# The opening of a three-layer decoder kernel: the attention pipeline filled by the rounds of its own loop, or by a program written out for each engine

## What is computed

```
x = LN(x + attn(x))        # LN, QKV, rotary; A = sum over tokens of l2(K)*V; Y = A*l2(Q); Y @ W_out + x
x = LN(x + xattn(ctx, x))  # 16 heads of 64: queries from x, keys and values from LN(ctx) and LN(x), softmax, @ Wo
x = LN(x + ffn(x))         # 8 experts of width 512, each token goes to its top 2
```

## Time and profile before

| | |
|---|---|
| time, three executions | 1606.64 us median (1605.07 to 1608.68) |
| profiled execution | 1606.26 us, span 1604.4 us |
| PE busy | 1432.5 us, 89% |
| DVE, ACT, POOL busy | 1105.5, 1031.7, 904.7 us |
| first matmul, first scores of tile 0 | 5.72 us, 76.38 us after the start of the span |

### The profile page before, as it was taken

How to read it: one execution, slowest core, us unless ns; L and a number is a source line. 1 busy time by engine, 2 the same in 40 slices (tenths; PEclk the granted TensorE clock), 3 DMA queues, 4 the chain that set the end, 5 groups by cost and what they waited for, 6 DMA issues and landing times.

```text
span 1604.4 us, 36488 instructions
## 1 busy us (share of the span) xinstructions
PE 1432.5 (89%) x10509; PEld 1239.7 (77%) x10509; DVE 1105.5 (69%) x4107; ACT 1031.7 (64%) x3827; POOL 904.7 (56%) x1233
## 2 busy tenths in 40 slices
PE   5699999999999999999999999999997499999940
PEld 4578888888888888888888888888886498889940
DVE  3366777767777677776777767777666588777865
ACT  2377776777767777677776777767764255555535
POOL 3355556665566665666556665566544255455565
PEclk9799999999999999999999999999999699999975
DMA  2000000000000000000000000000000676677746
GB/s 78 11 11 8 15 16 15 18 16 15 16 15 18 17 14 16 15 18 17 14 16 15 17 17 14 16 16 17 10 10 14 181 242 218 213 221 225 222 153 196
DMA packets 64624, 96.18 MB, mean 60 GB/s; under 512 B 10892, under 2 KB 48786, under 8 KB 64306
## 3 DMA queue, kind: packets, MB, share of 16 engines
q1 hardware_dynamic: 44738, 71.90, 15.0%
q0 software_dynamic: 8896, 16.94, 3.1%
q10 hardware_dynamic: 10800, 5.06, 1.2%
HBM read 71.55 MB, written 23.35 MB: 59 GB/s over the span
## 4 chain that ended last, share of the span: by engine, by line
PE 69%; DVE 10%; ACT 9%; DMA 4%; issue 4%; POOL 2%; SPq 2%; ACTq 0%; POOLq 0%; DVEq 0%
PE ps_s L1208 15%; PE ps_o L1221 11%; PE ps_t L1241 10%; ACT probs L607 6%; PE ps_pT L1231 5%; PE ps_t L1371 3%; PE ps_u L1256 3%; PE ps_a L1307 3%; PE ps_u L1258 3%; PE ps_u L1257 3%; DVE neg_max L759 3%; DVE pT L771 3%; PE ps_u L1371 2%; DVE k_pick L814 2%; DMA f_x<-x_rows 2%
## 5 line engine op out<-in xcount | busy, mean ns | idle before, releaser
L607 ACT ACTIVATE probs<-ps_s,neg_max 128x128 f32<-128x128 f32 x1024 | 361.8, 366 | 290.2 <-DVE neg_max L759 290.2
L496 POOL TENSOR_TENSOR probs_n<-probs,inv_sum 128x512 f32<-128x512 f32 x256 | 265.9, 1039 | 251.6 <-DVE inv_sum L765 249.6
L1208 PE MATMUL ps_s<-kvT,u_sb 128*128 128x128 f32 x2048 | 281.1, 280 | 0.0
L1208 PEld LDWEIGHTS ps_s<-kvT,u_sb 128*128 128x128 f32 x2048 | 255.2, 192 | 33.2 <-issue 31.8
L1241 PE MATMUL ps_t<-pT,kv_rows 128*128 128x512 f32 x512 | 262.2, 594 | 0.8 <-DVE pT L771 0.8
L1221 PE MATMUL ps_o<-value_w,tT 128*128 128x128 f32 x2048 | 260.5, 275 | 2.4 <-ACT tT L618 2.2
L759 DVE TENSOR_REDUCE neg_max<-ps_s 128x4 f32<-128x512 f32 x256 | 176.2, 688 | 103.9 <-PE ps_s L1208 103.4
L1221 PEld LDWEIGHTS ps_o<-value_w,tT 128*128 128x128 f32 x2048 | 244.0, 192 | 4.3 <-ACT tT L618 4.3
L553 POOL DMA_INDIRECT y_rows<-wvT,f_id x144 | 144.8, 1006 | 152.4 <-DVE wvT L1118 94.9
L607 ACT ACTIVATION_READ_ACCUMULATOR probs<-ps_s,neg_max 128x1 f32 x1024 | 208.2, 203 | 0.0
L508 POOL DMA_INDIRECT x_rows<-routed,pos_i x128 | 136.7, 1068 | 121.2 <-DVE pos_i L950 101.0
(11 more groups left out here) (237 smaller groups left out, 3165.6 us busy)
## 6 DMA issues: line engine op xcount, KB each, us to landing
u_sb<-in_expert_w SPq DMA_DIRECT2D x45, 578.0 KB
tT<-in_expert_w SPq DMA_DIRECT2D x27, 578.0 KB
f_x<-x_rows SPq DMA_DIRECT2D x72, 130.0 KB
tT<-y_rows SPq DMA_DIRECT2D x16, 512.0 KB, 4.7
x_raw<-in_x SPq DMA_DIRECT2D x64, 64.0 KB, 1.8
c_raw<-in_ctx_in SPq DMA_DIRECT2D x64, 64.0 KB, 2.0
out<-u_sb ACTq DMA_DIRECT2D x16, 256.0 KB, 2.4
y_rows<-wvT,f_id POOLq DMA_INDIRECT x144
```

Source lines behind the costliest of these rows:

```text
L496: nc.gpsimd.tensor_tensor(probs_n[:, sl], probs[:, sl], inv_sum[:, sl, :].rearrange("p (u o) -> p u o", o=1).to_broadcast([P, UP, P]), ALU ...
L607: last = nc.scalar.activation(probs[:, sl, j], ps_s[sl][:, j * P:(j + 1) * P], ACT.Exp, bias=neg_max[:, sl, j:j + 1], accum_out=sums[:, sl ...
L1208: last = nc.tensor.matmul(ps_s[sl][:, j * P:(j + 1) * P], u_sb[:, c // 2, BT * p + b, h:h + 2].rearrange("p h s -> p (h s)"), kvT[:, c, 2 ...
```

## The change

The periods start at t = 0. What the periods -5 to -1 did is written out, per engine, as one list of calls. In the lists, tiles 0 and 1 are treated side by side, then 2 and 3, then 4. To allow it, odd tiles below 5 (`FILL`) use `ps_o` in place of `ps_a`, tiles 2 and 3 use `ps_pT` for `KVT`, and the first eight latents parts alternate between `ps_u` and `ps_t`. The preparation jobs use five banks in place of seven and are strewn between the steps of the tiles. The score weights are split straight from the bank: ACT writes score_hi, DVE score_lo with one operation per job, in place of `split_scores`. The buffers for x and context are four each, their first loads stand in front of the large weights, and each constant has a semaphore that is awaited where it is first used. In the periods that remain three waits are new: `keep_qkv` for `sq_done`, `ctx_hat` for `kvT_ps`, and on PE `turn_latents` for `kvT_done` and `turn_rows_back` for `kv_done`; the wait for `score_split` is gone.

```diff
+        X_RING = 4
+        x_raw = sb("x_raw", [P, X_RING, D])
+        c_raw = sb("c_raw", [P, X_RING, D])
...
+        def chain_bank(j):
+
+            return ps_o if j < FILL and j % 2 else ps_a
...
+        def KVT(j):
+            return (ps_pT if 2 <= j < 4 else ps_u)[:, 0:BT * P]
+
+        def U_BANK(n):
+            return ps_t if n < 8 and n % 2 else ps_u
...
-        FIRST, LAST = -5, NT + 4
...
-            for t in range(FIRST, LAST + 1):
+            for t in range(LAST + 1):
...
+        ACT_JOBS = [0, 2, 4, 6, 7, 8, 9, 10, 11, 13]
+        DVE_JOBS = [1, 3, 5, 7, 8, 9, 10, 12, 14]
...
-            def load(j, q):
-                sp.wait_ge(z1_done, count(j - 1))
-                sp.wait_ge(c_hat_done, count(j - 1))
+            def load(j):
+                q = j % X_RING
+                sp.wait_ge(z1_done, count(j - (X_RING - 1)))
+                sp.wait_ge(c_hat_done, count(j - (X_RING - 1)))
                 sp.dma_start(x_raw[:, q:q + 1, :], x_t[one(j), :, :].rearrange("t p d -> p t d")).then_inc(x_in[q], 16)
...
             sp.dma_start(ident[:], eye).then_inc(s_ident, 16)
+            load(0)
             sp.dma_start(wq_raw[:], w_q).then_inc(s_wq, 16)
+            load(1)
             sp.dma_start(wkv_raw[:], w_kv).then_inc(s_wkv, 16)
-            load(0, 0)
             sp.dma_start(wo_raw[:], w_o.rearrange("(c p) n -> p c n", p=P)).then_inc(s_wo, 16)
-            sp.dma_start(tri[:], before).then_inc(s_const, 16)
-            sp.dma_start(eids[:], expert_ids).then_inc(s_const, 16)
-            sp.dma_start(rbase[:], region_base).then_inc(s_const, 16)
-            sp.dma_start(tids[:], tile_ids).then_inc(s_const, 16)
+            load(2)
+            load(3)
+            sp.dma_start(tri[:], before).then_inc(s_place, 16)
+            sp.dma_start(eids[:], expert_ids).then_inc(s_place, 16)
+            sp.dma_start(rbase[:], region_base).then_inc(s_place, 16)
+            sp.dma_start(tids[:], tile_ids).then_inc(s_place, 16)
...
+            load(4)
+            load(5)
...
+                if on(t, 6):
+                    load(t + 6)
...
+            def ctx_hat(j):
+                q = j % 2
+                pool.wait_ge(in_rstd, j + 1)
+                pool.wait_ge(kvT_ps, count(j - 1))
+                nc.gpsimd.tensor_scalar(c_hat[:, q], c_raw[:, j % X_RING], mv_in[:, q, 1, 0:1], rs_in[:, q, 1:2],
+                                        ALU.subtract, ALU.mult).then_inc(c_hat_done, 1)
...
             pool.wait_ge(half_set, 7)
-            pool.wait_ge(s_const, 16 * N_CONST)
-            pool.wait_ge(s_gains, 16 * N_GAINS)
+            in_rstds(0)
+            in_rstds(1)
+            ctx_hat(0)
+            ctx_hat(1)
+            qk_rstds(0)
+            qk_rstds(1)
+            in_rstds(2)
+            z1_rstds(0)
+            latent_hat(0)
+            z1_rstds(1)
+            latent_hat(1)
+            in_rstds(3)
+            qk_rstds(2)
+            ctx_hat(2)
+            ctx_hat(3)
+            z1_rstds(2)
+            qk_rstds(3)
+            latent_hat(2)
+            in_rstds(4)
+            z1_rstds(3)
+            latent_hat(3)
+            ctx_hat(4)
+            qk_rstds(4)
...
+                elif kind == "m":
+                    nc.scalar.activation(heads_of(g, score_hi[:]), bank[:].rearrange("p (c d) -> p c d", c=4), ACT.Copy,
+                                         scale=QS_SCALE).then_inc(prep_act, 1)
...
-            act.wait_ge(s_const, 16 * N_CONST)
-            act.wait_ge(s_gains, 16 * N_GAINS)
-            act.wait_ge(g_lat_set, 1)
```

ACT's list, which follows the definitions of its helpers:

```diff
+            keep_prepared(0)
+            act.wait_ge(s_norm, 32)
+            x_turned(0)
+            keep_prepared(2)
+            x_turned(1)
+            keep_qkv(0)
+            keep_prepared(4)
+            keep_qkv(1)
+            keep_prepared(6)
+            keep_prepared(7)
+            keep_prepared(8)
+            x_turned(2)
+            keep_prepared(9)
+            keep_qkv(2)
+            x_turned(3)
+            keep_prepared(10)
+            act.wait_ge(s_lat, 64)
+            act.wait_ge(g_lat_set, 1)
+            keep_kvT(0)
+            keep_prepared(11)
+            keep_qkv(3)
+            keep_kvT(1)
+            keep_prepared(13)
+            keep_u(0)
+            keep_rows(0)
+            keep_u(1)
+            keep_rows(1)
+            keep_u(2)
+            x_turned(4)
+            keep_u(3)
+            keep_u(4)
+            keep_qkv(4)
+            keep_u(5)
+            keep_kvT(2)
+            keep_u(6)
+            keep_u(7)
+            keep_kvT(3)
             periods(act, period)
```

DVE's split of the score weights, and its list:

```diff
+                if kind == "m":
+                    dve.wait_ge(prep_act, ACT_JOBS.index(at) + 1)
+                    nc.vector.scalar_tensor_tensor(heads_of(g, score_lo[:]), bank[:].rearrange("p (c d) -> p c d", c=4), QS_SCALE,
+                                                   heads_of(g, score_hi[:]).bitcast(F32), ALU.mult, ALU.subtract).then_inc(prep_dve, 1)
+                    return
...
+            stats(0)
+            stats(1)
+            in_hats(0)
+            keep_prepared(1)
+            in_hats(1)
+            dve.wait_ge(s_lat, 64)
+            nc.vector.tensor_scalar(g_lat[:], g_lat[:], (1 + EPS_LN) ** -0.5, None, ALU.mult).then_inc(g_lat_set, 1)
+            keep_prepared(3)
+            dve.wait_ge(s_rot, 48)
+            rotate(0)
+            keep_prepared(5)
+            pick(0)
+            rotate(1)
+            scale_queries(0)
+            stats(2)
+            pick(1)
+            residual(0)
+            keep_prepared(7)
+            scale_queries(1)
+            in_hats(2)
+            x1_norm(0)
+            residual(1)
+            keep_prepared(8)
+            stats(3)
+            x1_norm(1)
+            in_hats(3)
+            rotate(2)
+            keep_prepared(9)
+            pick(2)
+            keep_prepared(10)
+            split_latents(0)
+            rotate(3)
+            scale_queries(2)
+            keep_prepared(12)
+            split_latents(1)
+            keep_prepared(14)
+            residual(2)
+            pick(3)
+            stats(4)
+            x1_norm(2)
+            scale_queries(3)
+            in_hats(4)
+            residual(3)
+            dve.wait_ge(s_gate, 32)
+            dve.wait_ge(s_place, 64)
+            nc.vector.tensor_copy(tri_bf[:], tri[:]).then_inc(pad_ready, 1)
+            rotate(4)
+            x1_norm(3)
+            pick(4)
+            split_latents(2)
+            scale_queries(4)
             periods(dve, period)
```

PE's waits, two helpers and its list:

```diff
                 if at == TURNED:
-
-                    pe.wait_ge(prep_act, (TURNED + 1) // 2)
-                    pe.wait_ge(prep_dve, TURNED // 2)
+                    for kept in range(1, 5):
+                        pe.wait_ge(*prep_kept(kept))
+                if at == TURNED + 4:
...
-            for at in range(TURNED):
-                prepare(at)
-            pe.wait_ge(pad_ready, 5)
-            pe.wait_ge(s_const, 16 * N_CONST)
-            pe.wait_ge(s_gains, 16 * N_GAINS)
...
+            def latents_part(n):
+
+                pair = n // 8 % 2
+                if n % 4 == 0:
+                    tiles = min(n // 4 + 2, NT) if n >= 8 else 2
+                    pe.wait_ge(lT_done, tiles)
+                    pe.wait_ge(kvT_done, 3 * tiles)
+                pe.wait_ge(u_done, n if n >= 8 else count(n - 1))
...
+            def turn_latents(j):
+                pe.wait_ge(l_hat_done, j + 1)
+                pe.wait_ge(c_hat_done, j + 1)
+                pe.wait_ge(kvT_done, 3 * j)
+                nc.tensor.transpose(KVT(j)[:, 0:P], l_hat[:, j % 2], ident[:])
+                last = nc.tensor.transpose(KVT(j)[:, P:2 * P], c_hat[:, j % 2], ident[:])
+                last.then_inc(kvT_ps, 1)
+
+            def turn_rows_back(j):
+                pe.wait_ge(kv_done, min(j, 2))
...
+            prepare(0)
+            turn_x(0)
+            prepare(1)
+            pe.wait_ge(win_kept, 1)
+            make_qkv(0)
+            prepare(2)
+            turn_x(1)
+            prepare(3)
+            make_qkv(1)
+            prepare(4)
+            prepare(5)
+            prepare(6)
+            turn_queries(0)
+            prepare(7)
+            turn_queries(1)
+            pe.wait_ge(prep_act, 1)
+            project(0)
+            prepare(8)
+            project(1)
+            prepare(9)
+            turn_x(2)
+            make_qkv(2)
+            turn_x(3)
+            prepare(10)
+            turn_latents(0)
+            prepare(11)
+            make_qkv(3)
+            turn_queries(2)
+            turn_latents(1)
+            prepare(12)
+            prepare(13)
+            project(2)
+            prepare(14)
+            turn_queries(3)
+            for kept in range(TURNED, len(jobs)):
+                pe.wait_ge(*prep_kept(kept))
+            latents_part(0)
+            turn_rows_back(0)
+            latents_part(1)
+            project(3)
+            latents_part(2)
+            turn_rows_back(1)
```

(12 more changed lines are left out.)

528 lines of the change are left out of this document (259 added, 269 removed).

## The result

| | before | after |
|---|---|---|
| median (5 runs each) | 1608.52 us (1605.07 to 1611.18) | 1600.05 us (1597.65 to 1600.47) |
| ratio, 95% interval | | 0.9942 (0.9917 to 0.9968) |
| profiled execution | 1606.26 us | 1598.73 us, span 1596.9 us |
| first scores of tile 0 | 76.4 us | 61.2 us |

The account below looks back on a forecast made before the run. PE idles in the fill, each step waiting for another engine. First scores 15.7 us earlier, or 18.7 with the clock up; 17.2 taken, so 1606.6 - 17.2 = 1589.4 us, range 1582 to 1599.

Parts of the forecast that it names:

- the length of the new fill: Start to first scores of tile 0: forecast to end at 60.7 us, 15.7 earlier than 76.4.
- `turn_queries(0)`: End of the fill's first stretch: expected at 17.1 us, after the QKV of tile 0 and `pick(0)`.
- The first latents part: End of the fill's middle stretch: 17.1 + 20.0 of PE work + 7.6 of waits, so 44.7 us.
- The wait ahead of `turn_queries(3)`: PE in the middle stretch: 4.7 us lost to queued residual, roots and `pick(3)` on DVE and POOL.
- From the first latents part to the scores: Last stretch of the fill: 14.4 us of steps, 0.6 waiting for `pick(4)`, 0.95 for last result and copy.
- an even chance: Stretch from 44.7 us: even chance its second half runs at 2.4 GHz, saving 1.5 us net there.
- the steady period: The 64 periods: new waits cost 0, period stays 18.23 us; bound 0.28 us per period either side.
- rivals 4 and 5: 4: `turn_rows_back` lengthens periods, 1607 (chance 0.04) or 1614 (0.03). 5: period 0 gives gains back, 1605 (0.02).
- the further 1.5 us that a faster clock was to save in period 0: Period 0, whose first unit ran slow before: another 1.5 us saved if the clock rises in the latents.
- Rival 3: Middle stretch: clock rises in the products, PE's 20.0 us shrink to 10, some 6 us more, 1583; chance 0.12.
- the profiled execution was 1606.3, near the median 1606.6: Total time: profiled execution near the median; forecast subtracted 17.2 from 1606.6, giving 1589.4 us.
- whatever moves the first scores moves the end by as much: Behind the first scores: their shift reaches the end in full, if the period stays 18.23 us.

Follow-up runs that it names:

- the second bank: Changed kernel with 16 tiles, all eight latents parts of the fill put through ps_u, so without alternating banks: first scores at 65.4 us, median 1378.15 us.
- the execution with 68.6: Kernel before, cut to 16 of the 72 expert tiles, first run: first scores at 68.6 us, median 1382.61 us.
- that with 73.4: Kernel before, cut to 16 of the 72 expert tiles, run again: first scores at 73.4 us, median 1385.87 us.
- the cast on ScalarE: Changed kernel with 48 added transposes, cast of the rows' upper part moved from VectorE to ScalarE: 1597.69 us, ratio 0.9938, tiles 287.9 us.
- with 16 tiles: Either kernel running 16 of 72 expert tiles, last stage adding input rows instead of experts' rows: before 1382.61 us, again 1385.87; changed 1376.34.
- added transposes: Kernel before with 16 tiles, 37 transposes of the identity added where TensorE waits in the fill: 1385.88 us, first scores at 69.8 us.
- Addresses: Kernel before with four slots for x_raw and c_raw, giving later buffers the changed kernel's SBUF addresses: ratio 0.9978, tiles 283.8 us.
- late rows: Either kernel with eight instead of four buffers for an expert tile's rows: ratio 1.0021 on the kernel before, 0.9949 on the changed kernel.

## Why the prediction was right and wrong

**Right in the total, by luck in part: the length of the new fill.** First scores at 60.7 forecast, 61.2 to 62.7 in the four traces with the new fill as it is. The parts inside were off. `turn_queries(0)` came at 19.7 and not at 17.1: I had VectorE go on with tile 0 once its rows were there, but its list puts `stats(1)` first, and the rows of tile 1 landed at 10.1. The first latents part came at 48.5 and not at 44.7. The wait ahead of `turn_queries(3)` was 4.3 us, forecast 4.7 (the terms that I named for it add up to 4.2). From the first latents part to the scores it was 12.7 and not 16.0, because the clock was up there from about 51.5 on, which I had given an even chance. The errors are of opposite sign, and so the total fits better than its parts: 3.8 late at the latents, 3.3 made good behind them. With the clock up in the latents I had asked for 59.2, so by its own terms the forecast was 2 us short.

**Right: the steady period.** 1147.9 us in both; rivals 4 and 5 did not occur. Nor did the further 1.5 us that a faster clock was to save in period 0: the gain is 15.2 at the first scores and 15.2 at the last. Rival 3, the clock rising in the products, occurred in part: it was up from 17.5 to 24 us and down again until about 51.

**Wrong: the step "the profiled execution was 1606.3, near the median 1606.6".** I took the 76.4 us of that execution for the fill of the kernel before. In six traces of the old fill the first scores came at 76.4, 73.2, 75.2, 68.6, 73.4 and 74.8, mean 73.6; in four of the new one at 61.2, 62.7, 61.7 and 61.3, mean 61.7. So the fill gained 11.9 us on the mean and 15.2 only against the slowest of them. The 76.4 was a fill with PE at its slow spacing nearly to the end, and I had written this down as a property of the kernel ("since the first 50 us of before ran so"). Side by side, two traces of the same program show the 2.4 GHz in one and the 1.2 in the other. That the total agreed with the median proved nothing, as a long fill and short tiles (279.0 us, the shortest of all) had cancelled in it.

The six traces also show where the gain lies. The first latents part comes at 46.7 to 50.9 in the old fill (mean 49.2) and at 47.9 to 49.2 in the new (48.6), which by then has turned the queries of four tiles and not of three. From there to the scores it is 24.4 us in the mean before and 13.2 after: nearly the whole gain shows behind the first latents part. Ahead of it, doing without the waits for `tids` and `l_hat` shows as one more tile under way. Of the 11.2 us behind it the second bank is worth 2.2 to 3.4 by its run; for the rest no run separates the clock from the work that is already done by then.

The page TensorE: Matmul & The Clock Gate of the Trainium skill, Part 1, says that sustained activity releases the half-rate clock. By that rule the old products would run fast; the traces agree in the execution with 68.6 and not in that with 73.4, so here it could be neither taken nor left.

**Wrong: the step "whatever moves the first scores moves the end by as much".** It holds up to the last scores. Behind them stand 72 tiles whose rhythm falls out differently each time: 279.0, 283.8, 279.9 and 286.3 us with the old fill (mean 282.3), 288.3, 281.3, 284.2, 282.7 and 288.5 with the new (285.0; five of these nine are kernels with an edit from the experiments above, and the 287.9 with the cast on ScalarE is left out). The means differ by 2.7 us with ranges of 7.3 and 7.2. I read that as chance, but it is not shown: with 16 tiles it was 63.2 and 63.1 us with the old fill (67.4 with added transposes) and 64.1 to 66.0 in seven kernels with the new one, so a part of it may follow from the change. The forecast of 17.2 then comes apart like this: 2.8 for the old fill (73.6 and not 76.4), 1.0 for the new one (61.7 and not 60.7), 1.5 for the clock term, which brought nothing beyond that, and 2.7 for the tiles, which leaves 9.2 us. That agrees with the 8.5 and 8.0 that were measured. My range left out the spread of a stage that I had not looked at.

**Still open** is what makes the paired rhythm. Addresses, late rows and the cast on VectorE were tried, and none made the tiles even. In it VectorE gets the result 3.0 us after its first matmul (1305.04 to 1308.06), in the even one 2.0 (1306.10 to 1308.09), though the matmuls follow each other at the same pace in both. What holds the signal up I can't say.

## What to carry to other kernels

Before a gain is reckoned against a profile, ask which part of that one execution could have come out differently. A stage in which PE's spacing changes level, or one with two rhythms, needs a second trace or a bound of its own; agreement of the total with the median doesn't tell that its parts are typical. A fill can be measured by itself when the varying stage behind it is cut short: the five times of the new fill then lay within 1.8 us and those of the old within 9, and that spread is a result too. Last, where the matrix engine has to wait in a fill anyway, matmuls that do no work can be worth 2 us, for they bring the clock up for the work right behind (0.36 us for a latents matmul in place of 0.56). In the old fill they left the median where it was (1385.88 and 1385.87 us), so the trace of the place has to show it.

## What was not expected of the hardware

- One program, two outcomes: at the same place of the old fill the products ran at 1.2 GHz in one execution and at 2.4 in another, with first scores at 73.4 and 68.6 us. PE had been busy without a break from 14.1 us in the one and 14.4 in the other. In three of the six traces it never rose in the 13 us that followed.
- The column of the granted clock reads 1.00 from the start of the span until the first fall in each trace (62 us in before, 24 in after), while the spacing of 0.21 us says 1.2 GHz in parts of it. In that stretch only the spacing tells the level.
- Issuing a transfer can take long in itself: the sixth load of rows took 4.09 us on the SyncE queue, with nine transfers ahead of it, where the first seven transfers took 0.4 each. In the other traces of the new order it took 3.1 to 4.4, and 2.3 with the weights in front:

```profile
4.99 1.64 SPq L402 DMA_DIRECT2D x_raw<-in_x  x1
6.67 4.09 SPq L404 DMA_DIRECT2D c_raw<-in_ctx_in  x1
10.86 0.39 SPq L402 DMA_DIRECT2D x_raw<-in_x  x1
```

- 72 equal tiles without a branch in the four engines' lists take from 279.0 to 288.5 us, in a mixture of two rhythms whose cause is open.
